# Signalling the products of a group of tiles by halves in two passes over the edges of a graph network

## The reference

```python
def _sage_layer(x, src, dst, Wl, Wr, bias, n_nodes):     # layers three to five; layer one is alike
    msg_sum = jax.ops.segment_sum(x[src], dst, num_segments=n_nodes)
    cnt = jax.ops.segment_sum(jnp.ones((src.shape[0], 1), x.dtype), dst, num_segments=n_nodes)
    mean = msg_sum / jnp.maximum(cnt, 1.0)
    return mean @ Wl + x @ Wr + bias
```

## Time and profile before

| | |
|---|---|
| median of 3 runs | 8128.8 us (8126.4 to 8131.12) |
| the profiled execution: its own time | 8131.45 us |
| its span in the trace | 8129.1 us |
| pass of layer one, first gather to the end of the last | 40 to 1045 us |
| pass of layer three with the adjacency steps | 2457 to 3436 us |
| layers four and five on the adjacency matrix | 3480 to 4580 us |
| attention layers | 4589 us to the end |

### The profile page before, as it was taken

One profiled execution on the slowest core, in us unless ns is written; L12 is line 12 of the kernel. 1 busy time (PEld: TensorE's weight loads), 2 busy tenths in 40 slices (PEclk: granted clock), 3 DMA queues, 4 the chain that ended last, 5 costly groups with the idle time before them and its releaser, 6 DMA issues.

```text
span 8129.1 us, 101857 instructions
## 1 busy us (share of the span) xinstructions
PE 5028.7 (62%) x25982; PEld 3325.4 (41%) x25982; DVE 5111.2 (63%) x17152; ACT 2001.6 (25%) x3703; POOL 4896.4 (60%) x5045
## 2 busy tenths in 40 slices
PE   5566556666547777699999872542673533754532
PEld 3444443333334444354444442542443533434532
DVE  7777567777659898810001396853697843787744
ACT  6666654443416666610000000000100000000000
POOL 5777747777647777600000377777677776777774
PEclk8877777777767888799999855765656756556756
DMA  6555557777515555588888623421233321234311
GB/s 177 165 156 152 155 156 198 200 204 198 146 36 198 204 206 200 203 280 290 279 292 289 193 74 117 120 68 37 71 112 108 117 55 39 78 115 121 94 52 32
DMA packets 728900, 1216.85 MB, mean 150 GB/s; under 512 B 109340, under 2 KB 547085, under 8 KB 714832
## 3 DMA queue, kind: packets, MB, share of 16 engines
q1 hardware_dynamic: 552716, 847.76, 31.3%
q0 software_dynamic: 161120, 311.32, 14.7%
q10 hardware_dynamic: 14688, 53.48, 1.7%
HBM read 865.31 MB, written 346.85 MB: 149 GB/s over the span
## 4 chain that ended last, share of the span: by engine, by line
POOL 45%; PE 20%; issue 18%; DVE 14%; ACT 1%; DMA 1%; DVEq 1%; SPq 0%; POOLq 0%; ACTq 0%
POOL RO L1021 24%; POOL RO L980 18%; PE PS L1546 13%; PE PS L1501 3%; DVE H L2405 2%; DVE shared L2112 2%; POOL nd L1003 2%; DVE acc L1982 2%; DVE cut_row L2112 2%; DVE bn L2111 2%; PE PS L1481 1%; DVE RO L2393 1%; PE PS L1659 1%; POOL at_first L996 1%; DVE RO L1958 1%
## 5 line engine op out<-in xcount | busy, mean ns | idle before, releaser
L1021 POOL DMA_INDIRECT RO<-table,src_t x2346 | 2244.6, 957 | 2000.6 <-DMA table<-H 1244.4
L980 POOL DMA_INDIRECT RO<-table,src_t x2346 | 2309.3, 984 | 1021.0 <-issue 744.2
L1982 DVE TENSOR_TENSOR acc<-acc,PS 128x128 f32 x3910 | 1093.4, 280 | 1156.0 <-PE PS L1586 755.0
L1586 PE MATMUL PS<-RO 128*128 128x128 f32 x3060 | 683.4, 413 | 1174.7 <-DMA RO<-table,src_t 1151.1
L1586 PEld LDWEIGHTS PS<-RO 128*128 128x128 f32 x3060 | 631.4, 314 | 1219.2 <-DMA RO<-table,src_t 1196.7
L2211 DVE TENSOR_SCALAR RO<-PS,loc_t,shared 128x128 f32<-128x128 f32 x2346 | 940.4, 402 | 0.6
L1501 PE MATMUL PS<-RO 128*128 128x128 f32 x3128 | 623.4, 381 | 400.9 <-DMA RO<-table,src_t 386.3
L1501 PEld LDWEIGHTS PS<-RO 128*128 128x128 f32 x3128 | 599.8, 291 | 486.3 <-DMA RO<-table,src_t 461.5
L1286 ACT ACTIVATE small<-small 128x49 f32<-128x49 f32 x3 | 0.7, 245 | 2017.9 <-DVE small L2457 2017.9
L1146 ACT ACTIVATE H<-PS 128x392 f32<-128x392 f32 x784 | 392.4, 501 | 385.4 <-PE PS L1481 376.0
L1659 PEld LDWEIGHTS PS<-als_bf,RO 128*128 128x128 bf16 x7056 | 308.3, 119 | 426.8 <-DVE RO L2393 269.8
(11 more groups left out here) (403 smaller groups left out, 8833.3 us busy)
## 6 DMA issues: line engine op xcount, KB each, us to landing
GT<-adjacency SPq DMA_DIRECT2D x126, 1792.0 KB, 7.2
adjacency<-H SPq DMA_DIRECT2D x98, 1568.0 KB
RO<-adjacency SPq DMA_DIRECT2D x42, 1792.0 KB, 7.2
RO<-table,src_t POOLq DMA_INDIRECT x4692, 3.1
staged<-RO ACTq DMA_DIRECT2D x102, 512.0 KB
H<-staged SPq DMA_DIRECT2D x102, 512.0 KB
soft_rows<-shared SPq DMA_DIRECT2D x196, 256.0 KB
H<-soft_rows SPq DMA_DIRECT2D x98, 512.0 KB, 3.9
```

Source lines behind the costliest of these rows:

```text
L980: pool.indirect_dma_start(rows[:, h * HT + j, :], None, table[k % 2], at(src_t[:, t:t + 1]))\
L1021: pool.indirect_dma_start(rows[:, g % 2 * HT + j, :], None, table[k % 2], at(src_t[:, t:t + 1]))\
L1586: last = mm(PS[:, o:o + D], block[:, j * D:(j + 1) * D], onehot[:, h * HT + j, :], start=True, stop=True)
L1982: tt(at, at, window_at(k, c, j), ALU.add).then_inc(added[h], 1 if j < n - 1 else HT - n + 1)
```

## The change

In layers one and three `multiplied[h]` now rises twice a group, at the fourth tile and at the eighth. VectorE waits for the first rise before the adds of tiles 0 to 3, and for the second before those of tiles 4 to 7. GpSimd waits before tile 0 until the first four slots of its group are free, and before tile 4 until all are. Everywhere else (the attention layers, group 97) the semaphore rises by two at once, and all the counts that are waited for are doubled.

```diff
-        def multiplied_by(k, c):
-
-            return multiplied[c % 2], c // 2 + 1 + turn[k] * ITERS
+        def multiplied_by(k, c, halves=2):
+
+            return multiplied[c % 2], 2 * (c // 2 + turn[k] * ITERS) + halves
@@ GpSimd, gathers(i, h)
-                    else:
-                        wait(pool, multiplied[h], i + turn[k] * ITERS)
                     g = 2 * i + h
                     for j in range(real_tiles(g)):
                         t = g * HT + j
+                        if k != 1 and j % LH == 0:
+                            free = 2 * (i + turn[k] * ITERS)
+                            wait(pool, multiplied[h], free if i == 0 or j else free - 1)
@@ GpSimd, attention layers
-                        pool.wait_ge(multiplied[g], turn[k] * ITERS)
+                        pool.wait_ge(multiplied[g], 2 * turn[k] * ITERS)
@@ TensorE, edge_pass
-                    last.then_inc(multiplied[h], 1)
+                        if c < NG - 1 and j == LH - 1:
+                            last.then_inc(multiplied[h], 1)
+                    last.then_inc(multiplied[h], 1 if c < NG - 1 else 2)
@@ TensorE, weighted_pass
-                    last.then_inc(multiplied[h], 1)
+                    last.then_inc(multiplied[h], 2)
@@ VectorE, add_group
-                    v.wait_ge(*multiplied_by(k, c))
+                    v.wait_ge(*multiplied_by(k, c, 2 if k in GAT else 1))
                 for j in range(n):
-                    if c == NG - 1 and j == LH:
+                    if j == LH and (c == NG - 1 or k not in GAT):
                         v.wait_ge(*multiplied_by(k, c))
```

## The result

| | kernel before | changed kernel |
|---|---|---|
| median, on the same chip | 8127.6 us (8125.9 to 8131.12, 4 runs) | 8066.3 us (8064.23 to 8077.71, 4 runs) |
| ratio, 95% interval | | 0.9929 [0.9916, 0.9943] |
| span of the profiled execution | 8129.1 us | 8065.2 us |
| first to last adjacency step | 2437.5 to 3442.4: 1004.9 us | 2424.3 to 3381.1: 956.8 us |

The change saves 61.3 us between the medians; 55.6 us were forecast (8073 us). The same kernel was run once more, on another chip, and gave 0.9917 [0.99, 0.9933].

A forecast was written before the change was run, and what follows sets the result against it. Layer one was taken as bound by GpSimd's gathers, layer three by VectorE's work and its waits for products; 50 + 4 + 1.6 = 55.6 us off gave 8073 us on the median's scale, 8 in 10 for 8050 to 8105.

The forecast's parts named there:

- part 2: Layer three, GpSimd refills by halves: its own work is a floor of 911.1 us; 10 us taken off, 50 remain.
- Part 1: Layer three, VectorE adds after four tiles: gains up to 1.15 us per wait until the ring stalls it, 60.2 us.
- Does it stay?: Layer three: the gain lasts, since TensorE's late last steps, after 2.48 us idle, wait for VectorE and move forward with it.
- collisions: Layer three: GpSimd's floor and VectorE's loop both bind at times, costing 10 us of the gain, range 0 to 20.
- Part 3: Ahead of the steps, 2280 to 2457 us: about five VectorE waits for products each lose 0.9 us, 4 us.
- Part 4: Layer one: GpSimd's single 1.72 us wait for TensorE, ahead of the gather at 83.80, goes; 1.6 us off.
- Part 5: The added waits on VectorE and GpSimd cost nothing when met: 0 us, upper bound 0.24 us per GpSimd wait.
- rival D: Layer one: GpSimd's added waits cost 0.24 us each, 23 us; kernel slower at 8146 if layer three gains little; chance 0.04.
- Rival A: Layer three: one-hots delay 49 more gathers, raising GpSimd's floor by 39 us; 35 us off, 8094; chance 0.15.
- Rival B: Layer three: TensorE's clock rises, matmuls shrink and VectorE's wait goes whole; 73.5 us off, 8055; chance 0.14.
- Rival C: Layer three: VectorE starts earlier but stalls at the ring, so the wait only moves; 8123, no change; chance 0.09.

The follow-up runs named there:

- run 25: Not a label: 25 counts gathers of 1.6 us or more in the unedited changed kernel's second run, 8060.95 us against the kernel before's 8125.85, ratio 0.9917.
- the PSUM one-hots: Changed kernel with layer three's one-hots from group 11 on built against column numbers in PSUM; against the kernel before 1.002, 1.0022 and 1.0005, all on 9500 us chips.

## Why the prediction was right

The total is nearer than its parts. Between the spans 63.9 us went and 55.6 were forecast. The steady part of layer three was put at 50 and gave 48.2, by two errors that cancel (part 2); the stretch ahead of the steps was put at 4 and gave 8.6, what lies before layer three at 1.6 and gave 4.5, the rest at 0 and gave 2.6. The mechanism, VectorE starting earlier until the ring and GpSimd's floor stop it, is what the traces of the 8130 us chips show.

**The bound before** was read rightly: VectorE's waiting for L1501 was what could be had, and the stage shrank by what VectorE's idle time and its masks lost.

**Part 1, the size of a wait.** Its stall at the third pair of masks was put at some 0.6 us and is 0.56 us in the group shown. Waits left: some 37 us expected (97.4 - 60.2), 38.4 measured. But the 38.4 us are not the leftovers that I meant, with none of them for late rows: TensorE itself now waits some 28 us for gathered rows, and VectorE behind it. The agreement of the two numbers is partly chance.

One reading under "Does it stay?" was wrong. The 2.48 us of idle time ahead of TensorE's last two steps, at 2846.17, were put down to VectorE ("that delay starts when VectorE has delivered"), as the row names a mask. But the masks of these two steps were written by 2844.01. What filled the time is the load of eight registers on TensorE's own queue, before:

```profile
L1473 PEldq TENSOR_LOAD <-GT x1: 2017/2017/2017, 2843.4 to 2843.4; - x1
```

It starts when the step before has started and takes 2.02 us, whatever VectorE does. All 39 of TensorE's gaps over 2 us ahead of a step stand at such a load, and so do the 57 of the changed kernel. The 196 loads take 186 us in all before and 215 after (median 0.59 us in both, the longest 2.08 and 2.25). So the change didn't shorten this part of TensorE's loop, it grew by some 30 us, and the gain held all the same; why some loads take over three times as long as others no run shows.

**Part 2, the mis-sized term: GpSimd's floor.** "Without its waits for TensorE the stage cannot be shorter than 979 - 67.9 = 911.1 us." This took the 54 waits whole. A gap between two gathers is 0.30 us where nothing is waited for, and this gap lies inside each of the 54: 54 x 0.30 = 16.2 us can't go. The floor is 979 - 51.7 = 927.3 us, above the 918.8 us of VectorE's loop, not below. On this scale the stage measured 979 - 48.2 = 930.8 us: 3.5 us above the corrected floor. So GpSimd's pass runs at its own floor, and no collisions on top of the two limits are needed to explain the stage: the 10 us guessed for them came out near the truth (60.2 - 48.2 = 12) by luck, because the floor's error had that size. That both limits "will bind at times" is borne out in so far as the chain still runs over VectorE's loop in part of the stage (3100 to 3300 us above). GpSimd from the first step to the last, before:

```profile
L980 POOL DMA_INDIRECT RO<-table,src_t x698 | 712.1, 1020 | 274.1 <-issue 206.2 <-PE PS L1501 67.9
```

and after:

```profile
L981 POOL DMA_INDIRECT RO<-table,src_t x698 | 715.2, 1025 | 226.1 <-issue 225.8 <-PE PS L1502 0.3
```

The wait of 67.9 us went, yet the idle time fell by only 48.0: "issue" rose by 19.6 us, 16.2 us of it gaps that were booked to TensorE and are now booked to nobody. The evidence that GpSimd is the main bound on the 8130 us chips is that it waits for nobody in the whole stage but for 0.3 us (1.3 in the second trace), and that the chain of the stage lies 83% on it (74%). It is read from the traces; no experiment on such a chip tested it.

**Part 3**, ahead of the steps: 4 us expected, 8.6 measured. The waits from the pass's first matmul to the tenth group, before (2272 to 2446 us):

```profile
POOL RO L980 <- PE PS L1501: 67.8, 6, 22.1
DVE acc L1982 <- PE PS L1501: 62.5, 7, 12.7
```

and after (2268 to 2433 us):

```profile
POOL RO L981 <- PE PS L1502: 59.1, 6, 19.7
DVE acc L1985 <- PE PS L1502: 54.6, 8, 11.6
```

GpSimd's waits for products fell by 8.7 us there, as much as the stretch shrank, and VectorE's by 7.9. I had priced VectorE's half groups alone, and left out that GpSimd's refill too no longer stands behind the whole group.

**Part 4**, layer one: 1.6 us expected. GpSimd's one wait of 1.72 us became

```profile
82.79 0.94 POOL L981 DMA_INDIRECT RO<-table,src_t  x1 [0.71 <-PE PS L1502]
```

1.0 us earlier. The half of the group comes later than half of its 3.44 us. The pass lost 3.5 us (1004.0, now 1000.5) and in the second run of the changed kernel 5.8 (998.2); the difference to 1.0 is in GpSimd's irregular gaps, which differ from run to run. On VectorE the adds of a group are now in two pieces in layer one, with 0.20 us between them, off the path:

```profile
1038.86 1.55 DVE L1985 TENSOR_TENSOR acc<-acc,PS 128x128 f32 x4 [0.29 <-issue]
1040.60 1.55 DVE L1985 TENSOR_TENSOR acc<-acc,PS 128x128 f32 x4 [0.20 <-DVE acc L1985]
```

**Part 5 and rival D**: nothing for the met waits. In the timeline above, whose five gathers must hold at least one that carries a wait, every gap on GpSimd is 0.30 us, as in the earlier trace rows. On VectorE 0.2 us of the adds' idle time stand behind "issue" in layer three.

**Rival A** (one-hots meet more gathers) fell: gathers of 1.6 us or more in the whole pass of layer three were 39 and are 31, in the second run 25. The mechanism is real, but its count didn't grow when GpSimd stopped idling.

**Rival B** holds in a small part: the granted clock of the stretch rose from 0.80 to 0.82 of full, a mean between the levels of 1.2 and 2.4 GHz, and the product matmuls of the steps' stretch take 368 ns on average in the changed kernel's profile and 357 in its second, against 382 before. Over 1404 matmuls the 14 ns of the first are 19 us of TensorE's time; whether the earlier start would have brought 48 us without them no run separates. The waits did not go whole.

**Rival C** is false on the 8130 us chips; on the 9500 us chips its outcome, no change that can be told, is the measured one, with most of the gain taken back at the ring. The 0.09 given to it was for the chip of the profile; on the others it would have been the right forecast. What decides between the two was not found.

**Left open:** which of the two edits carries the 48 us on the 8130 us chips, since each alone ran only on the others; why the refill alone costs over 100 us there; whether the PSUM one-hots would give time where GpSimd is the bound. The untested rival is that the adds alone, or the refill alone, would give the whole gain on an 8130 us chip.

## What to carry to other kernels

When an engine's idle time is split by what ended it, the wait that can be taken away is the row's total less the ordinary gap times its count; here 67.9 us were worth 51.7, and this put GpSimd's floor above VectorE's loop. Look also at the queue's own instructions in such a gap: a row named a mask for 2.48 us of idle time that was a register load of 2.02 us. Before signalling earlier, find the next thing that the woken engine needs from the same partner (here a ring slot behind the second half of the matmuls): the gain is the time up to that point, here put at 1.15 us of a 3 us wait. After such a change look for the engine that had slack of the same size as the gain: GpSimd's was 52 us, and the stage shrank by 48. And a gain on one chip need not be one on another: on the 9500 us chips the same edits gave nothing.

## What was not expected of the hardware

**Two kinds of chips.** The kernel before takes 8126 to 8128 us on some chips and 9438 to 9516 on others, run after run. Not every stage differs: layers four and five, where TensorE is busy throughout, take 1095 us on either kind (3485 to 4580 us before, 4013 to 5107 in the kernel with halves in layer one only). Over the whole kernel the granted clock is 0.73 of full on the first and 0.68 to 0.69 on the second. A register instruction of TensorE's queue, ahead of every step, tells them apart (shortest, median, longest in ns). Kernel before on an 8130 us chip:

```profile
L1481 PEldq FUSED_REGOPS  x1567: 88/90/118, 2437.5 to 3442.4; - x196
```

and the kernel with halves in layer one only on a 9500 us chip:

```profile
L1482 PEldq FUSED_REGOPS  x1567: 3/90/1394, 2865.9 to 3970.2; - x196
```

The median is the same, but single ones take up to 1394 ns, an instruction that moves no data. The same traces have idle time ended by "remote", as in the rows of the experiments, of which the traces on the 8130 us chips show none at all. Gathers themselves are no slower there (median 946 ns with halves in layer three only, 954 in the changed kernel on an 8130 us chip). What stops the engines was not found, nor whether the lower clock is a cause or follows from the stops.

**A comparison whose one operand is in PSUM didn't delay the gathers here**, the same one with both in SBUF did: 0.94 against 1.73 us for the gather that starts during it, at 1.20 and 1.21 us of the one-hot.

**A load of eight registers on TensorE's queue took between 0.59 and 2.27 us** on the 8130 us chips, and the rows of idle time don't name it: they book the gap to the semaphore that came last, or to "issue".
